# Rotary attention: keys for eight heads, scores in two 64-row strips, and the maximum taken off by VectorE in even slots

## The reference

```python
# 16 heads of 8; q, k, v = x @ Wq, ctx @ Wk, ctx @ Wv, split in heads
q = apply_rope(rms_norm(q, q_norm_w), cos32, sin32)
k = apply_rope(rms_norm(k, k_norm_w), cos1000, sin1000)
scores = einsum("bhqd,bhkd->bhqk", q, k) * 8 ** -0.5     # 128 x 77 for each head
p = softmax(scores, axis=-1)
y = einsum("bhqk,bhkd->bhqd", p, v).merge_heads() @ Wo
```

## Time and profile before

| | before |
|---|---|
| median of 3 runs | 3026.99 us |
| the profiled execution's own time | 3017.08 us |
| its span, first to last instruction | 3015.3 us |
| mean granted TensorE clock | 0.965 of 2.4 GHz |
| PE, DVE, ACT, POOL busy | 91%, 60%, 69%, 48% |
| rotary stage, its exponentials | 2061.2 to 2599.0 us |

### The profile page before, as it was taken

The page is one execution under the profiler, slowest core; times in us unless marked ns, Lnnn a source line. Parts: engine busy times, 40 slices in busy tenths (PEclk is TensorE's granted clock), DMA queues, the critical chain, the costliest instruction groups (busy, mean ns, idle before and its releaser), DMA issues. The chain is left out here.

```text
span 3015.3 us, 69304 instructions
## 1 busy us (share of the span) xinstructions
PE 2737.1 (91%) x21504; PEld 1982.6 (66%) x21504; DVE 1805.1 (60%) x5293; ACT 2070.9 (69%) x7235; POOL 1460.1 (48%) x1978
## 2 busy tenths in 40 slices
PE   8999999999999956998799999978999999699987
PEld 6666777777777746998355555546776666458874
DVE  6883344443444444554688888876677776444545
ACT  6766778777787743443699999976888888522224
POOL 3442224444444454555433333325678887724665
PEclk9999999999999987999899999998999999799998
DMA  9910030220400402221310000000000010001225
GB/s 264 338 47 15 19 116 16 80 78 20 129 27 20 135 30 72 73 70 57 115 56 10 9 10 8 10 22 10 13 27 28 29 31 17 29 26 56 80 79 185
DMA packets 179960, 185.08 MB, mean 61 GB/s; under 512 B 32844, under 2 KB 168537, under 8 KB 179216
## 3 DMA queue, kind: packets, MB, share of 16 engines
q1 hardware_dynamic: 162032, 145.14, 16.1%
q0 software_dynamic: 17280, 34.13, 3.4%
q10 hardware_dynamic: 288, 1.38, 0.2%
HBM read 58.34 MB, written 111.48 MB: 56 GB/s over the span
## 5 line engine op out<-in xcount | busy, mean ns | idle before, releaser
L678 POOL TENSOR_TENSOR wide_probs<-wide_exps,wide_inv_sum 128x308 f32<-128x308 f32 x256 | 179.3, 700 | 488.9 <-DVE wide_inv_sum L1409 486.0
L1400 DVE TENSOR_REDUCE wide_neg_max<-banks 128x4 f32<-128x308 f32 x256 | 122.5, 478 | 473.6 <-PE banks L982 448.9
L1116 ACT ACTIVATE causal_exps<-causal_biased,causal_neg_max 128x128 f32<-128x128 f32 x1024 | 325.8, 391 | 31.1 <-DVE causal_neg_max L1400 29.7
L1119 ACT ACTIVATE wide_exps<-banks,wide_neg_max 128x77 f32<-128x77 f32 x1024 | 315.8, 326 | 0.3 <-DVE wide_neg_max L1400 0.2
L658 POOL DMA_INDIRECT sorted_x<-send,place_i x240 | 244.9, 1020 | 96.0 <-issue 40.5
L1116 ACT ACTIVATE rotary_exps<-banks,rotary_neg_max 128x77 f32<-128x77 f32 x1024 | 252.0, 351 | 15.1 <-DVE rotary_neg_max L1400 13.7
L1103 ACT ACTIVATE wide_probsT<-banks 77x512 f32<-77x512 f32 x256 | 152.1, 594 | 153.6 <-PE banks L991 149.5
L1656 ACT ACTIVATE gelu_hidden<-banks,gelu_slot 128x256 f32<-128x256 f32 x284 | 116.7, 471 | 157.3 <-PE banks L1833 153.1
L1587 POOL DMA_INDIRECT results<-swiglu_tile_out,swiglu_dest_i x142 | 147.7, 1040 | 141.2 <-DVE swiglu_tile_out L1738 97.8
L1119 ACT ACTIVATION_READ_ACCUMULATOR wide_exps<-banks,wide_neg_max 128x1 f32 x1024 | 213.9, 209 | 0.0
L1587 POOL DMA_INDIRECT results<-gelu_tile_out,gelu_dest_i x142 | 140.8, 991 | 142.3 <-DVE gelu_tile_out L1743 119.0
(11 more groups left out here) (382 smaller groups left out, 7339.3 us busy)
## 6 DMA issues: line engine op xcount, KB each, us to landing
sorted_x<-blank SPq DMA_DIRECT2D x1, 34848.0 KB, 116.8
sorted_x<-blank SPq DMA_DIRECT2D x4, 8712.0 KB, 30.3
gelu_tile_in<-sorted_x SPq DMA_DIRECT2D x71, 132.0 KB
swiglu_tile_in<-sorted_x SPq DMA_DIRECT2D x71, 132.0 KB
gelu_back<-results SPq DMA_DIRECT2D x16, 512.0 KB, 7.7
swiglu_back<-results SPq DMA_DIRECT2D x16, 512.0 KB, 6.2
X<-in_x SPq DMA_DIRECT2D x8, 512.0 KB, 7.3
regions<-in_g_w SPq DMA_DIRECT2D x2, 2048.0 KB, 20.9
```

What stands on the lines that cost most here:

```text
L678: pool.tensor_tensor(probs[:, m % SLOTS], exps[:, m % SLOTS], inv_sum[:, m % SLOTS].unsqueeze(2).to_broadcast([P, HU, NK]), ALU.mult).then ...
L1116: last = act.activation(exps[:, (NU * c.c + k) % ES, h], scores[:, h * NK:(h + 1) * NK], ACT.Exp, bias=neg_max[:, k % SLOTS, h:h + 1])
L1119: last = act.activation(exps[:, k % SLOTS, h], scores[:, h * NK:(h + 1) * NK], ACT.Exp, bias=neg_max[:, k % SLOTS, h:h + 1], accum_out=exp ...
L1400: dve.tensor_reduce(neg_max[:, k % SLOTS], scores.rearrange("p (h n) -> p h n", h=HU), AX.X, ALU.max, negate=True).then_inc(max_done, 1)
```

## The change

In the rotary stage alone:
- `keys` holds eight heads side by side across the 128 rows (KH = 8, a mask `heads8` that is the sum of the masks of heads 0 to 7 and 8 to 15), so POOL makes one tile of 128 x 308 for two slots. The lower and upper 64 rows of it belong to different heads.
- In an even slot PE issues both score matmuls of the slots k and k+1, each with 64 rows, into banks 0 and 1. It waits first for the exponentials of slot k-1 and for the subtraction of slot k-2. In odd slots it issues none.
- In an even slot DVE takes the maximum of slot k (not negated), the negated maximum of slot k+1, and then subtracts the first from the scores of slot k into a new SBUF buffer `biased`. In odd slots it does none of this.
- ACT takes one exponential of 128 x 308 from `biased` in even slots, and four of 128 x 77 from the bank, with the bias, in odd ones.
- `exps` has four buffers in place of three; the order of the heads in the slots changes to that of the causal stage.

The code of the other two kinds is put in another order and issues the same instructions.

```diff
-    ES = 4 if kind == "causal" else 3 if late else SLOTS
-    BS = 4
-    KH = 8 if kind == "causal" else H
+    ES = 4 if late else SLOTS
+    BS = 4 if kind == "causal" else 2
+    KH = 8 if late else H
...
-            return 8 * (j % 2) + 4 * (j // 2) if kind == "causal" else HU * j
+            return 8 * (j % 2) + 4 * (j // 2) if late else HU * j
...
-                engine.wait_ge(s_ps, pair.back(1).count(NU, 2 * piece + 2 if kind == "causal" else piece + 1))
+                engine.wait_ge(s_ps, pair.back(1).count(NU, 2 * piece + 2))
...
+                        if late and k % 2 == 0:
+                            pe.wait_ge(keys_done[k // 2 % 2], c.count(2, k // 4 + 1))
+                            if before(c, k, 1) is not None:
+                                bc, bk = before(c, k, 1)
+                                if kind == "causal":
                                     pe.wait_ge(biased_done, bc.count(NU, bk + 1))
+                                else:
+                                    pe.wait_ge(biased_done, bc.count(OG, bk // 2 + 1))
+                                    pe.wait_ge(exps_done, bc.count(NU, bk + 1))
+                            for n in range(2):
+                                rows = slice(64 * n, 64 * n + 64)
+                                pe.matmul(s_bank[n][:, 0:HU * NK], qT[rows, c.c % 2, b], keys[rows, b, HU * (j // 2):HU * (j // 2) + HU],
+                                          start=True, stop=True).then_inc(s_ps, 1)
...
+                        level = kind == "rotary" and k % 2 == 0
+                        if level:
+                            act.wait_ge(biased_done, c.count(OG, k // 2 + 1))
+                        else:
+                            act.wait_ge(max_done, c.count(NU, k + 1))
...
+                        if level:
+                            last = act.activation(exps[:, (NU * c.c + k) % ES].rearrange("p h n -> p (h n)"), scores, ACT.Exp)
...
+            def find_top(c, k):
+                dve.wait_ge(s_ps, c.count(NU, k + 1))
+                if before(c, k, SLOTS) is not None:
+                    bc, bk = before(c, k, SLOTS)
+                    if k % 2 == 0:
+                        dve.wait_ge(biased_done, bc.count(OG, bk // 2 + 1))
+                    else:
+                        dve.wait_ge(exps_done, bc.count(NU, bk + 1))
+                dve.tensor_reduce(neg_max[:, k % SLOTS], s_bank[k % 2][:, 0:HU * NK].rearrange("p (h n) -> p h n", h=HU), AX.X,
+                                  ALU.max, negate=k % 2 == 1).then_inc(max_done, 1)
+
+            def take_top(c, k):
+                dve.wait_ge(max_done, c.count(NU, k + 1))
+                if before(c, k, 2 * BS) is not None:
+                    bc, bk = before(c, k, 2 * BS)
+                    dve.wait_ge(exps_done, bc.count(NU, bk + 1))
+                dve.tensor_tensor(biased[:, k // 2 % BS].rearrange("p (h n) -> p h n", h=HU),
+                                  s_bank[k % 2][:, 0:HU * NK].rearrange("p (h n) -> p h n", h=HU),
+                                  neg_max[:, k % SLOTS].unsqueeze(2).to_broadcast([P, HU, NK]), ALU.subtract).then_inc(biased_done, 1)
...
+                    if c is not None and kind == "rotary" and k % 2 == 0:
+                        find_top(c, k)
+                        find_top(c, k + 1)
+                        take_top(c, k)
```

## The result

The changed kernel takes 3183.41 us (four runs, 3179.23 to 3188.15) against 3027.63 for the kernel before on the same chip: a ratio of 1.0516, 95% interval 1.0497 to 1.0535, 156 us slower. The profiled execution has a span of 3177.3 us and a mean granted clock of 0.947.

The account below looks back on a forecast made before the run. PE (95% busy) was taken to bound the rotary stage. Loop 18.2, ACT's other work 2.5 and waits 0.5 make 21.2 us a pair against 16.8; 32 pairs add 141, giving 3158, plus 10 is 3168 us; range 3105 to 3210.

Parts of the forecast that it names:

- closed loop: Rotary stage, two slots: scores wait for slot k-1's exponentials, closing a loop of 4.54 us against 4.20 now.
- steps 1 to 4: Loop from ACT's end through PE's scores and DVE to the even exponential: 0.15, 0.85, 1.43, then 0.04 + 0.46 us.
- Step 3: DVE's part of the loop: maximum of k, maximum of k+1, subtraction, 0.475 + 0.475 + 0.48 = 1.43 us.
- The 0.5 us for further waits: Per pair: ACT waiting for PE's late transposes in slots 1, 5, 7, and DVE late at slot 4; between 0 and 1.5.
- the loop without waits: Rotary stage: four loops, 18.2 us, plus 2.5 us of ACT's other work on the path, 20.7 us a pair.
- rival C: Clock falls because PE idles before even slots; whole rotary stage at 1.2 GHz gives +14 us a pair, 3480; 3%.
- C's sign: A granted clock under 0.95 in the rotary stage would show that the clock had fallen.
- What I wrote of ACT: Rotary stage: ACT waits for DVE's subtraction in nearly every even slot; 2.4 us a pair of waiting hides its other work.
- the reading in the prediction: Skill's rule read as strip pair taking as long as one matmul: sum 13 to 26 us lower; the row was preferred.
- Rival A: Faster: the loop is hidden, PE stays the bound and its saving counts, 41 to 51 us, about 2981; 8%.
- rival B: Strips don't overlap at 308 columns: two full matmuls, 0.36 us more four times a pair, +46 us, 3214; 3%.
- rival D: The two effects cancel, within 0.2% or 6 us of now; needs a loop of 16.8 us; 2%.

Follow-up runs that it names:

- e9: Kernel before, full-height scores kept, with only the subtraction and the single exponential in even slots; 3034.31 us, ratio 1.0024.
- e10: Kernel before with even-slot subtraction and single exponential, plus both full-height scores issued together behind slot k-1's exponentials; 3212.47 us, ratio 1.0606.
- e1: Changed kernel, but PE issues one 64-row score matmul in each slot and waits only for its own bank; 3166.15 us, ratio 1.0485.
- e7: Changed kernel with four dummy full-height matmuls ahead of PE's wait in every even rotary slot; 3148.56 us, ratio 1.0406.
- e6: Changed kernel with DVE's subtraction and a single exponential in every slot, PE waiting for the subtraction alone; 3083.06 us, ratio 1.0188.
- e3: Changed kernel with DVE's order turned to maximum of k, subtraction of k, maximum of k+1; ratio 1.0498.
- e4: Changed kernel with PE's transposes of slot k-2 moved ahead of the wait for the scores in even slots; ratio 1.0449.
- e11: e1 with one dummy full-height matmul ahead of the scores of every slot; 3124.67 us on another chip, ratio 1.0453.
- e14: Changed kernel with DVE's subtraction before the second maximum, PE's transposes of slot k-2 before the wait, and two dummy matmuls in even slots; ratio 1.0382.

## Why the prediction was right

The forecast, slower by a closed loop, 3168 us, met 3183; the range held it. Step by step:

Most durations of steps 1 to 4 came out as taken: hand-over 0.14 us (0.15), score start to DVE 0.84 in the turn shown and 0.91 on average (0.85), strip pair 0.72 (0.68, with 0.72 as its end), subtraction 0.469 (0.48), single exponential 0.459 (0.46). Step 3 as a whole did not: from the start of the first maximum to the end of the subtraction are 1.26 us in the turn shown, 1.25 on average, where the sum had 1.43, because the three instructions overlap a little (2404.55 + 0.86 ends after 2405.34). That is 0.7 us a pair too much in the forecast. The groups by line of the changed kernel, 2110 to 2730 us:

```profile
L1376 DVE TENSOR_TENSOR rotary_biased<-banks,rotary_neg_max 128x308 f32<-128x308 f32 x114 | 53.5, 469 | 0.0
L1111 ACT ACTIVATE rotary_exps<-rotary_biased 128x308 f32<-128x308 f32 x114 | 52.1, 457 | 8.0 <-DVE rotary_biased L1376 3.2
```

The wait as the cause: shown. e9 to e10 adds it, with the common issue that it belongs to, +174 us in the stage; e1 without it runs through more slots than e7 with it at the same clock; e6 takes it out, -100, with the shorter exponentials beside it.

The 0.5 us for further waits was named rightly and mis-sized. I added up the changed kernel's trace between the ends of the exponentials of two odd slots, for the pairs in the middle of the stage, where a pair takes 21.9 us:

| us a pair | forecast | changed | e7, clock 1.00 |
|---|---|---|---|
| exponentials' end to scores | 0.6 | 0.6 | 0.7 |
| scores' start to DVE | 3.4 | 3.6 | 3.4 |
| two maxima and the subtraction | 5.7 | 5.0 | 5.0 |
| subtraction's end to ACT, even exponential | 2.0 | 2.3 | 2.0 |
| copy of `probsT` and four exponentials, odd slots | 6.4 | 6.2 | 6.2 |
| ACT's other work between them | 2.5 | 2.5 | 2.5 |
| further waits (measured: ACT in odd slots for PE's transposes) | 0.5 | 1.7 | 1.1 |
| sum | 21.2 | 21.9 | 20.9 |

The late transposes are there, in slots 1, 5 and 7 as forecast (0.47, 1.01 and 0.22 us, none in slot 3), and cost 1.7 us a pair. Of the 1.0 us that e7 gives back, 0.6 are this wait: the lower clock makes PE's list longer, and ACT waits for it. The forecast came near because step 3 was 0.7 too long and the waits 1.2 too short. That the loop without waits, 20.7, is also what e7 shows (659.5 / 32 = 20.6) is luck of the same kind. In rival C I treated the lower clock as something for the whole stage, with 3%, and the forecast had no term for it. The clock was 0.91, under the 0.95 that I had named as C's sign; the truth was the forecast with a little of C in it. The row of the causal stage that I leaned on had its strips, but no wait for ACT's exponentials ahead of them.

What I wrote of ACT was half right: it does stand idle in even slots, but for the transposes and not for the subtraction (3.2 us). The 190.3 us of its wait for transposes are about three quarters in even slots and the rest in odd ones. I had hidden `probsT` of slot k-2 in ACT's wait for the scores, and overlooked that its transposes are issued behind those scores. It cost nothing in the sum, as in even slots the two ways are of about one length: e3 and e4 showed both.

The Trainium skill ("TensorE: Matmul & The Clock Gate", Part 3, Measured speedup vs the span model) says that each further row group adds about 4 ns. The trace agrees: a pair holds PE for 0.719 us and a single strip for 0.711 to 0.713, 6 to 8 ns less. What failed is the reading in the prediction, that by this rule a pair takes as long as one full-height matmul: the first strip alone takes 0.1 to 0.2 us more than that (0.52 to 0.62). The row decided rightly about the pair's length, and the reason was not the second strip.

Rival A fell (PE 79% busy), rival B fell (the pair takes what one strip takes), rival D fell.

## What to carry to other kernels

When two slots are issued together, look who empties the last bank: if it is the engine at the end of the chain, the double buffer is gone and the stage runs at the length of the loop, however much work was taken off every engine. Add that loop up from the trace, both ways round, before counting what each engine saves. And take the granted clock as a term of the sum wherever TensorE gets less to do or waits more.

## What the hardware showed that I had not expected

- A 64-row fp32 matmul of 308 columns holds PE for 0.71 us alone and 0.72 in a pair, a 128-row one for 0.52 to 0.62; the weight load of the transposes behind the pair starts with them and not ahead of them (2404.43 for both in the timeline above), where before it started 0.26 us ahead (2304.05 in the trace of before, for the transposes that start at 2304.31 in the earlier trace rows).
- With 64-row scores and PE busy all the time the granted clock stayed at 0.50 for the first 87 us of the stage (e1). In full height it was 1.00 between 2070 and 2470 us (e9). With full-height dummies in PE's idle time it went from 0.91 to 1.00 (e7).
- DVE's `root_part` product (L1191, 128 x 128) took 0.48 us on average before and 0.65 after, its neighbour L1193 went from 0.88 to 0.39. The medians hardly differ (0.31 and 0.28, 0.35 and 0.28): a few long ones, up to 2.6 us, make the averages. Why was not tested.
- On the two chips of e11 to e14 the kernel before takes 2988.6 and 2988.7 us, 38 less than on that of e6 to e10. The last stage of these kernels is shorter there: the first matmuls of its experts run over 199 us in e11 to e14 and over 232 to 233 in e6, e7, e9 and e10, with the same code.
